# Softmax denominators of an attention kernel: TensorE's pass of ones and GpSimd's scaling against transposing sums, a round trip by DRAM and a scaling on VectorE

## The reference

```python
xn = layernorm(x)                                   # x: 4 x 2048 x 512
q, k, v = heads(xn @ q_w.T + q_b) / sqrt(32), heads(xn @ k_w.T + k_b), heads(xn @ v_w.T + v_b)
attn = softmax(einsum('bhqd,bhkd->bhqk', q, k))     # 2048 x 2048 for each of 64 (batch, head)
ctx = einsum('bhqk,bhkd->bhqd', attn, v)
out = x + (merge(ctx) @ out_w.T + out_b) + tanh(xn @ w @ a1 @ a2 + ffn_b)
```

## Time and profile before

| what | us |
|---|---|
| median of three runs | 4121.41 (4121.28 to 4122.97) |
| the profiled execution: time / span of its instructions | 4121.45 / 4119.6 |
| its busy time: PE, POOL, DVE, ACT | 4060.4, 3243.9, 3122.5, 2357.2 |

### The profile page before, as it was taken

How to read it: one execution, slowest core, us unless ns; L and a number is a source line. 1 busy time by engine, 2 the same in 40 slices (tenths; PEclk the granted TensorE clock), 3 DMA queues, 4 the chain that set the end, 5 groups by cost and what they waited for, 6 DMA issues and landing times.

```text
span 4119.6 us, 77775 instructions
## 1 busy us (share of the span) xinstructions
PE 4060.4 (99%) x21280; PEld 2484.5 (60%) x21280; DVE 3122.5 (76%) x5058; ACT 2357.2 (57%) x4515; POOL 3243.9 (79%) x1172
## 2 busy tenths in 40 slices
PE   8999999999999999999999999999999999999999
PEld 6888888755555555555555555555555555555467
DVE  4344334788888888888888888888888888888654
ACT  2222222266666676766666666676666666676731
POOL 1222222289999999999999999999999999999940
PEclk9999999999999999999999999999999999999999
DMA  4444445578888888888888888878888888888767
GB/s 171 163 163 163 153 150 169 160 149 171 175 177 178 171 175 172 172 171 172 174 175 177 172 174 171 174 167 176 176 174 176 171 170 172 170 176 171 155 232 263
DMA packets 245346, 714.79 MB, mean 174 GB/s; under 512 B 87280, under 2 KB 88304, under 8 KB 184432
## 3 DMA queue, kind: packets, MB, share of 16 engines
q0 software_dynamic: 54288, 395.34, 49.6%
q1 hardware_dynamic: 107648, 201.88, 14.5%
q10 hardware_dynamic: 83040, 113.01, 9.8%
HBM read 178.00 MB, written 136.31 MB: 76 GB/s over the span
## 4 chain that ended last, share of the span: by engine, by line
PE 46%; DMA 19%; issue 10%; ACT 3%; POOL 2%; POOLq 0%; ACTq 0%; DVE 0%; DVEq 0%
PE sm_bank L1086 13%; PE pv_bank L1117 13%; PE st_bank L1111 13%; DMA dma_sum<-pool_sum 10%; DMA dma_sum<-probs 9%; PE sm_bank L281 3%; ACT probs L905 3%; PE sm_bank L1117 2%; PE st_bank L281 1%; POOL pool_sum L819 1%; POOL ctx_out L844 1%; POOL dma_sum L830 0%; PE sm_bank L1095 0%; PE sm_bank L1111 0%; ACTq L904 0%
## 5 line engine op out<-in xcount | busy, mean ns | idle before, releaser
L991 DVE TENSOR_REDUCE part_max<-sm_bank 128x1 f32<-128x512 f32 x4016 | 2440.5, 676 | 421.6 <-PE sm_bank L1086 415.4
L819 POOL TENSOR_TENSOR pool_sum<-pool_sum,probs 128x2048 f32<-128x2048 f32 x504 | 2462.7, 4886 | 17.6 <-ACT probs L905 2.2
L905 ACT ACTIVATE probs<-st_bank 128x512 f32<-128x512 f32 x3810 | 1946.7, 616 | 605.2 <-PE st_bank L1111 577.6
L1086 PE MATMUL sm_bank<-k_stack,q_stack 96*128 96x512 f32 x4016 | 1654.1, 412 | 5.2 <-issue 2.6
L1111 PE MATMUL st_bank<-q_stack,k_stack 97*128 97x512 f32 x4064 | 1628.9, 402 | 11.7 <-ACT probs L905 5.4
L1086 PEld LDWEIGHTS sm_bank<-k_stack,q_stack 96*128 96x128 f32 x4016 | 762.1, 190 | 556.6 <-DVE part_max L991 334.0
L1117 PE MATMUL pv_bank<-probs,v_pairs 128*32 128x512 f32 x7680 | 933.6, 600 | 0.0
L1111 PEld LDWEIGHTS st_bank<-q_stack,k_stack 97*128 97x128 f32 x4064 | 772.2, 190 | 251.3 <-ACT probs L905 114.2
L1117 PEld LDWEIGHTS pv_bank<-probs,v_pairs 128*32 128x32 f32 x7680 | 202.9, 109 | 452.9 <-ACT probs L905 259.2
L830 POOL DMA_DIRECT2D dma_sum<-probs x315 | 342.6, 1088 | 70.1 <-ACT probs L905 28.9
L425 POOL TENSOR_TENSOR y_out<-y_out,x_in 128x512 f32<-128x512 f32 x64 | 82.8, 1293 | 370.1 <-ACT y_out L457 365.6
(11 more groups left out here) (126 smaller groups left out, 3267.1 us busy)
## 6 DMA issues: line engine op xcount, KB each, us to landing
dma_sum<-probs POOLq DMA_DIRECT2D x315, 1024.0 KB, 8.2
dma_sum<-pool_sum POOLq DMA_DIRECT2D x62, 1024.0 KB, 10.3
q_stack<-s_q_hi ACTq DMA_DIRECT2D x122, 256.0 KB, 6.1
k_stack<-s_k_hi ACTq DMA_DIRECT2D x122, 256.0 KB, 4.3
x_in<-in_x SPq DMA_DIRECT2D x16, 1024.0 KB, 7.7
s_q_hi<-qk_hi SPq DMA_DIRECT2D x16, 1024.0 KB, 4.3
s_q_lo<-qk_lo SPq DMA_DIRECT2D x16, 1024.0 KB, 6.4
s_k_hi<-qk_hi SPq DMA_DIRECT2D x16, 1024.0 KB, 4.3
```

Source lines behind the costliest of these rows:

```text
L819: nc.gpsimd.tensor_tensor(total[:], one[:], tile_at(r, kt)[:], ALU.add).then_inc(pool_added, 1)
L905: nc.scalar.activation(tile_at(r, kt)[:, q * BLK:(q + 1) * BLK], score_bank(h, kt * QB + q), ACT.Exp, scale=SCALE).then_inc(probs_ready, 1)
L991: nc.vector.tensor_reduce(part_max[:, k:k + 1], sm_bank[:, sm_place(k)], AX.X, ALU.max).then_inc(max_scores_read, 1)
L1086: nc.tensor.matmul(sm_bank[:, sm_place(k)], q_st[r][0:ROWS, q * P:(q + 1) * P], k_st[r][0:ROWS, b * BLK:(b + 1) * BLK], start=True, stop=T ...
```

## The change

The sum over partitions moves from PE to DVE. A transposing sum (`fold`) takes 512 columns of `dma_sum` and sums each group of 32 partitions; four of them (after the maxima 55, 63, 7 and 15) leave `folded`, 128 x 64. SP writes `folded` to DRAM and reads it back by four DMAs, so that the four groups of 32 partitions come to lie beside each other (`gather`). After maximum 31 DVE sums these four and inverts the 128 x 16 totals (`invert_folded`). After maximum 39 it spreads them by a transpose into a bank of `st_bank` that is left out of the ring for this, and multiplies the context (`scale_in_spare`). POOL's `scale`, PE's `add_up` and ACT's `copy_sums` go, for all heads but the last three, which keep a pass of ones (now 1/32, since `invert` sums 32 equal rows). The rings of the banks change with it: `st_bank` skipped a bank at units 22 and 44 and does so at unit 24 and at the end; `sm_bank` skips one at units 32, 48 and at the end.

```diff
-RECIPS = [63, 7, 15]
+FOLDS, INVERT = [55, 63, 7, 15], 31
+SCALED = 39
-SM_TURN = [*range(TURN_UNIT), "max", *range(TURN_UNIT, SUM_UNIT), "sum", *range(SUM_UNIT, UNITS), None, None]
+SM_TURN = [*range(TURN_UNIT), "max", *range(TURN_UNIT, 32), None, *range(32, 48), None, *range(48, UNITS), None]
-    return u + (u >= 22) + (u >= 44)
+    return u + (u >= ST_SKIP)
...
+            def gather(h):
+                sp.wait_ge(totals_ready, PRIME + h)
+                sp.wait_ge(fold_ready, PRIME + h * QB + QB)
+                sp.dma_start(dram["folded"], folded[:].rearrange("p q b -> p (q b)")).then_inc(fold_stored, DMA)
+                sp.wait_ge(fold_stored, h * DMA + DMA)
+                for q in range(QB):
+                    src = dram["folded"][:, q * (BLK // DH):(q + 1) * (BLK // DH)].rearrange("(g p) b -> p g b", p=DH)
+                    sp.dma_start(gathered[q * DH:(q + 1) * DH], src).then_inc(fold_loaded, DMA)
...
-            def scale(h, r):
-                pool.wait_ge(pv_copied, PRIME + h + 1)
-                pool.wait_ge(recip_ready, h * len(RECIPS) + len(RECIPS))
-                pool.wait_ge(context_stored[r % 2], PRIME + (h // 2) * (CTX_DMAS * DMA))
-                nc.gpsimd.tensor_tensor(ctx_out[r % 2][:], pv_copy[r % 2][:], ratio[:], ALU.mult).then_inc(context_ready, 1)
...
+                    if kt == CHAINS[0][0]:
+                            act.wait_ge(fold_ready, PRIME + h * QB - 2 * QB + q + 1)
...
+            def fold(h, r, piece):
                 if piece == 0:
+                    dve.wait_ge(joined[r % 2], landed(h, len(CHAINS[0])))
+                total = dma_sum[r % 2][:, piece * BLK:(piece + 1) * BLK]
+                nc.vector.tensor_reduce(folded[:, piece], total.rearrange("p (b j) -> p b j", j=DH), AX.X, ALU.add,
+                                        apply_transpose=True).then_inc(fold_ready, 1)
+            def invert_folded(h):
+                dve.wait_ge(fold_loaded, h * (QB * DMA) + QB * DMA)
+                nc.vector.tensor_reduce(totals[:], gathered[:].rearrange("p g b -> p b g"), AX.X,
+                                        ALU.add).then_inc(totals_ready, 1)
+                dve.wait_ge(totals_ready, PRIME + h + 1)
+                nc.vector.reciprocal(inverse[:], totals[:]).then_inc(inverse_ready, 1)
+            def scale(h, r, ratio):
+                dve.wait_ge(inverse_ready, h + 1)
+                nc.vector.transpose(ratio.rearrange("p (b j) -> p b j", j=DH),
+                                    inverse[:].unsqueeze(2).to_broadcast([P, BLK // DH, DH])).then_inc(ratio_ready, 1)
...
+                nc.vector.tensor_tensor(ctx_out[r % 2][:], pv_copy[r % 2][:], ratio, ALU.mult).then_inc(context_ready, 1)
+            def scale_in_spare(h, r):
+                dve.wait_ge(probs_ready, PRIME + h * UNITS + 2 * UNITS + SPARE_BEFORE + 1)
+                scale(h, r, st_bank[:, spare_place()])
...
+                    if u == SPARE_AFTER:
+                        pe.wait_ge(context_ready, PRIME + h - 1)
```

More of the change, by code:

```diff
@@ L121, with spare_place @@
 assert early_maxima(BLOCKS - 1, BLOCK_UNITS - 1)[-1] == HEAD_MAXIMA - 1 and UNITS < TURN_SLOT
-assert UNITS == 64 and len(SM_TURN) % SM_BANKS == 0 and st_slot(UNITS - 1) == 65
+def spare_place():
+    return SPARE_SLOT % ST_BANKS
+SPARE_BEFORE = max(u for u in range(ST_SKIP) if st_place(u) == spare_place())
+SPARE_AFTER = min(u for u in range(ST_SKIP, UNITS) if st_place(u) == spare_place())
+assert ST_SKIP % (2 * PER_TILE) == 0 and ST_SLOTS % ST_BANKS == 0 and SCALED + 1 == ST_SKIP + AHEAD * PER_TILE == BEGIN
+assert UNITS == 64 and len(SM_TURN) % SM_BANKS == 0 and st_slot(UNITS - 1) == ST_SLOTS - 2
 def adds_after(kt):
@@ L193, in _ @@
             nc.gpsimd.memset(keep["ident"][:], 0.0).then_inc(ident_ready, 1)
-            nc.gpsimd.memset(keep["ones"][:], 1.0)
+            nc.gpsimd.memset(keep["ones"][:], 1.0 / DH)
             nc.gpsimd.memset(keep["power"][:], -0.5)
@@ L670, in build_attend @@
         last_sum = sm_bank[:, sm_place("max")]
-        out_banks = [sum_bank] + [sm_bank[:, b] for b in range(SM_BANKS) if b not in (sm_place("sum"), sm_place("max"))]
+        out_banks = [sum_bank] + [sm_bank[:, b] for b in range(SM_BANKS) if b not in (SUM_PLACE, sm_place("max"))]
         out_banks += [st_bank[:, 0]]
@@ L674, in build_attend @@
         end_ring = [st_place(END_TILE * QB + i) for i in range(ST_BANKS)]
-        end_ring += [ST_BANKS + b for b in range(SM_BANKS) if b not in (sm_place("sum"), sm_place("max"))]
+        end_ring += [ST_BANKS + b for b in range(SM_BANKS) if b not in (SUM_PLACE, sm_place("max"))]
         assert len(out_banks) == JT and BLK == DIM
@@ L779, in body @@
                         load_y(n, n)
+                if more >= 3:
+                    gather(h)
                 if more >= 1:
@@ L942, in body @@
                     exps(h, r, kt)
+                    if more == 1 and kt == END_TILE + 1:
+                        copy_sums(h - 1, (r - 1) % GROUP)
                     if kt in LOAD_AT and more >= GROUP - 1:
@@ L951, in body @@
                             load(h + GROUP, r, LOAD_AT.index(kt))
-                        if kt == CUT - 1:
+                        if kt == CUT - 1 and more == 1:
                             copy_sums(h, r)
@@ L1001, in begin, with rest @@
                     maxima(s, k, units, sums_of)
-            def rest(s, units=True, sums_of=None, last=False):
-                for k in range(BEGIN, UNITS):
-                    maxima(s, k, units, None if last else sums_of)
+            def rest(s, units=True, sums_of=None, begin=BEGIN):
+                for k in range(begin, UNITS):
+                    maxima(s, k, units, sums_of)
                 if units:
@@ L1011, in _ @@
             dve.sem_inc(max_row_ready, 1)
-            rest(1)
+            rest(1, begin=AHEAD * PER_TILE)
             begin(2)
@@ L1038, in body @@
                 elif more == 2:
-                    rest(following + 1, last=True)
+                    rest(following + 1)
                     negate(following + 1)
-                    for piece in range(len(RECIPS)):
-                        recip(h, r, piece)
+                    invert(h, r)
+                    scale(h, r, sum_bank)
                 elif more == 1:
```

80 lines of the change are left out of this document (44 added, 36 removed).

## The result

The changed kernel takes 4205.68 us (median of 4 runs, 4203.76 to 4222.82) against 4121.34 of the kernel before: a ratio of 1.0214, with a 95% interval of 1.0187 to 1.0241. It was forecast at 4063, faster; it is slower by 84 us. The profiled execution took 4207.42 us, with a span of 4205.6.

What follows compares the result with a forecast made beforehand. POOL was taken to set a head's time, held by its own work and a little by its DMAs: 4121.45 - 78 (scaling gone) + 20 (stores moved) = 4063 us, range 4005 to 4114.

Steps and rivals of the forecast that it cites:

- 78 us, if POOL goes on setting the time: POOL loses the scaling, 1.26 us of its order a head, from 62 heads: 78 us saved while POOL sets the pace.
- a little, by its own chain of DMAs: POOL idles 1.15 us of a 48.84 us head, ahead of a join, which also waits for the previous join's landing.
- the sign of being right: POOL's idle time per head would be 1.1 to 1.6 us, standing ahead of joins.
- the context's stores, +20 us: Stores move among first join, merge, second join: 0 to 0.67 us more POOL wait a head; 0.33 taken, 20 us.
- rival 2: DMAs of stores and round trip eat the saved time: 4121; chance 0.09, together with folds that bind DVE.
- The round trip: Store and four loads of folded sums through DRAM: 8.0 to 14.1 us, about 11 taken; up to 14.9 costs nothing.
- The slow rival: Round trip falls behind a second accumulating DMA, 19 us: 60 to 180 us slower, middle 4220; chance 0.14.
- The term's "zero": Cost of the DRAM round trip, taken as zero since DVE's idle time and POOL's room would cover it.
- folds at the lower end: On DVE a fold takes 0.6 to 0.7 us, not 1.2, so the additions are 4.2 us a head.
- DVE's own work, which stays below POOL's: DVE needs 43.6 to 47.0 us a head, lower end taken, against POOL's 47.6, so it costs nothing.
- where a few were forecast: The tail, where three heads keep the pass of ones, should differ by a few microseconds only.

Runs made afterwards that it cites:

- Run 5: The kernel before, with POOL's scaling in the loop cut from 512 columns to 8: 4101.87 us (0.9953).
- run 7: Changed kernel, PE's loop shifted by 96 instructions, round trip left out, context stores cut to 4 rows of 64, output projection fed from another tensor: 4108.3 us (0.9964).
- run 8: Changed kernel, complete, PE's loop shifted by 96 instructions, context stores issued one head later, behind the next round trip: 4128.17 us (1.0018).
- run 12: The kernel before, complete, with a head's four context stores held until POOL reaches the next head's merge: 4203.65 us (1.0202).
- run 1: Changed kernel with only PE's loop body shifted by 96 instructions among the fetched blocks: 4195.23 us (1.0178).
- run 4: Changed kernel, PE's loop shifted by 96 instructions, round trip's store and loads left out, totals taken of ones: 4164.53 us (1.0111).
- run 6: Changed kernel, PE's loop shifted by 96 instructions, a 128x512 product on an unread tile put back on POOL: 4235.97 us (1.0286).
- run 3: The kernel before with PE's loop moved by 187 instructions, so its closing branch is number 39 of its block: 4172.2 us (1.0112).

## Why the prediction was wrong

**The step that failed first: "78 us, if POOL goes on setting the time".** The condition did not hold. The prediction had read that POOL was held "a little, by its own chain of DMAs"; it treated that wait as a constant, and it is the buffer between two nearly equal bounds. Run 5 took 68 us of the term away in the kernel before and won 20; in the changed kernel POOL's idle time ahead of joins went from 0.91 to 3.43 us a head, where 1.1 to 1.6 were named as the sign of being right.

**The term that was mis-sized: the context's stores, +20 us.** The place was foreseen (among first join, merge and second join) and so was the victim. The price was worked out at the 394 GB/s of a quiet stretch; the queue's own share over the heads gives 0.9 us a head, and runs 7 and 8 measured 56 and 67 us, and run 12, in the kernel before and with the stores some 3 us earlier, even 85. With 1.26 us a head off POOL, the joins may also have come closer together; no run shows what that did. The first two failures are the mechanism of rival 2, to which the prediction gave 0.09 together with folds that bind DVE; but that rival stopped at no gain, and a loss was measured.

**What the prediction did not see: PE's branch.** It took 69 instructions out of PE's loop and counted only what they had cost. They had also stood between the start of a fetched block and the branch. It costs 10 us in the changed kernel, because POOL's waits cover most of it, 57 with the stores out of the way, and 51 in the kernel before.

**The round trip: right on time, wrong on price.** From the store's issue to the last landing it takes 9.3 us (median; 5.6 to 16.7), where about 11 was forecast, and DVE waits 9.4 us for it in all. The slow rival (a round trip behind a second accumulating DMA, 4220, though the middle of its 60 to 180 us is 4241) came near the measured time by another way, which is luck. The term's "zero" left out the 40,000 small packets, and its wait held only while PE lost time elsewhere (47.3 us in run 1): run 4 puts trip and wait together at 31 us.

A sum of the single measurements: 4121 - 20 (run 5) + 31 (runs 1 to 4) + 56 (runs 4 to 7) + 10 (the changed kernel to run 1) = 4198, against 4205.7. It is no proof, since the parts cover each other: branch and stores cost 77 us together and 10 or 21 when only one of them is taken away.

**Right:** folds at the lower end (0.70 us), and DVE's own work, which stays below POOL's. DVE is not off the path for that: its waits for the merge and the round trip hold PE's maxima, and what that costs no run shows. **Small:** of the 86 us between the two profiled executions, 74.6 lie between the first and the last merge (884.1 to 3868.5 us of the span before, 882.9 to 3941.9 after), but 12.6 behind the last one, where a few were forecast; that was not looked into. The Trainium skill ("DMA: Bandwidth & Descriptors", Queues, rings and completion order) lets queues share an engine packet by packet. No run here shows the packets' order; the 64 KB stores land after 2.5 us near the fifth join (run 8), 4.4 behind it in the kernel before, and 6.8 in the changed kernel, among first join, merge and second join.

**Open:** what PE's pass of ones was worth by itself, which no run tried; why a product on POOL costs two thirds of itself in run 6 but its removal in run 5 brought one third; what the low clock costs by itself; and why the same stores cost 56, 67 and 85 us in three kernels.

## What to carry to other kernels

Where the engine that sets the pace waits even a little for transfers, its work and the transfers are two bounds, and work taken off it is worth only the distance to the second: look for what then follows more closely. A store that moves is better priced by its queue's share of the DMA time in the busy stretch (here an estimated 0.9 us a head, 55 in all, against 56 to 85 measured), and by which landing the pace-setter waits for next, not by its bytes at the best rate. After any edit to a loop body, look at the branch that closes it: idle time "by issue" once a turn meant here that the code behind it was not there yet, and shifting the loop by some instructions (`head_slot`) took it away.

## What the runs showed of the hardware

A loop-closing branch of PE took 0.34 to 0.48 us where its block of 16 KB had been entered some 8 us before (kernel before), and 4.0 to 6.3 where it had been 2.6 (changed kernel); runs 1 and 3 turned each into the other by moving the loop. The same section of the Trainium skill on instruction fetch ("Runtime: NRT & Kernel Launch") says that a taken branch whose target isn't at hand forces a fetch before anything goes on; the runs agree, and add that here the branch's position in its block decided how much of that showed.

In a gap of 3.94 us in PE's work its granted clock fell to 0.50, and it stood there for 6.6 us, until 2053.5; the matmuls behind the gap took 0.63 us in place of 0.39. The clock was at 1.00 again in the window from 2054.0.
